# Two attention layers and two mixture-of-experts layers: shared expert's last 512 tokens behind the experts, tiles ordered by four levels, plain result rows

## What is computed

```python
scores = softmax(xt @ Wg.T)                      # 16 experts
# the 2 best of 4 groups, in them the 4 best experts of each token
h = silu(einsum('td,eid->eti', xt, W1)) * einsum('td,eid->eti', xt, W3)   # 176 inner values
y = einsum('etd,te->td', einsum('eti,edi->etd', h, W2), combine)
z = silu(xt @ Ws1.T) * (xt @ Ws3.T) @ Ws2.T      # shared expert, 352 inner values
x = x + y + z
```

## Time and profile before

| | us |
|---|---|
| median of 3 runs | 1341.67 |
| lowest, highest | 1340.03, 1342.01 |
| the profiled execution | 1353.53 |
| its span, first to last instruction | 1351.8 |
| TensorE busy | 1150.4 (85%) |
| VectorE busy | 876.2 (65%) |
| POOL busy | 688.8 (51%) |
| ScalarE busy | 541.6 (40%) |
| mean granted TensorE clock | 0.936 of full |

### The profile page before, as it was taken

The page is one execution under the profiler, slowest core; times in us unless marked ns, Lnnn a source line. Parts: engine busy times, 40 slices in busy tenths (PEclk is TensorE's granted clock), DMA queues, the critical chain, the costliest instruction groups (busy, mean ns, idle before and its releaser), DMA issues.

```text
span 1351.8 us, 26055 instructions
## 1 busy us (share of the span) xinstructions
PE 1150.4 (85%) x8706; PEld 615.6 (46%) x8706; DVE 876.2 (65%) x2067; ACT 541.6 (40%) x846; POOL 688.8 (51%) x841
## 2 busy tenths in 40 slices
PE   6888999998898899999287899999879878899990
PEld 2343444442654556566144344444247445565650
DVE  5578898991674345555389799999667524354543
ACT  2124777779520122222032477777844011222210
POOL 4352344444036577767453355454520656667671
PEclk9887999999988999999689899999998988899995
DMA  4424333320824679887745322121053347788868
GB/s 140 147 86 126 111 116 120 109 65 3 287 83 131 183 164 161 151 159 108 191 138 169 117 57 58 55 60 52 3 211 87 108 149 180 133 148 157 156 87 262
DMA packets 145875, 169.84 MB, mean 126 GB/s; under 512 B 20240, under 2 KB 130768, under 8 KB 145232
## 3 DMA queue, kind: packets, MB, share of 16 engines
q1 hardware_dynamic: 115856, 128.79, 32.8%
q0 software_dynamic: 29184, 38.36, 16.8%
q10 hardware_dynamic: 704, 1.02, 0.2%
HBM read 93.29 MB, written 76.18 MB: 125 GB/s over the span
## 4 chain that ended last, share of the span: by engine, by line
PE 57%; DVE 18%; DMA 7%; issue 6%; ACT 6%; SPq 2%; another core or an unknown queue 2%; POOL 2%; POOLq 0%; ACTq 0%; DVEq 0%
PE pair_ps L1992 10%; PE o_ps L1757 9%; ACT arena L845 4%; DVE nm L1119 4%; PE pair_ps L2025 4%; DMA x_slots<-y_sb,slot_i 4%; DVE bm L1119 3%; PE pair_ps L2028 2%; PE t_ps L1783 2%; PE pair_ps L1707 2%; PE pair_ps L1588 2%; PE pair_ps L1687 2%; PE pair_ps L1999 2%; PE pair_ps L1712 2%
## 5 line engine op out<-in xcount | busy, mean ns | idle before, releaser
L845 ACT ACTIVATE arena<-pair_ps 128x1024 f32<-128x1024 f32 x320 | 322.8, 1024 | 131.0 <-PE pair_ps L1682 76.1
L625 POOL TENSOR_SCALAR_AFFINE_SELECT arena<-arena 128x512 f32<-128x512 f32 (+1 forms) x320 | 174.9, 547 | 240.9 <-ACT arena L845 240.4
L1119 DVE TENSOR_REDUCE nm<-pair_ps 128x2 f32<-128x1024 f32 (+1 forms) x192 | 232.6, 1222 | 33.4 <-PE pair_ps L1731 29.6
L685 POOL DMA_INDIRECT x_slots<-y_sb,slot_i x128 | 123.9, 968 | 168.4 <-DVE slot_i L1317 89.9
L1757 PE MATMUL o_ps<-arena 128*9 128x512 f32 (+7 forms) x2048 | 177.0, 441 | 4.1 <-POOL arena L625 3.9
L1992 PE MATMUL pair_ps<-arena 128*128 x512 | 167.7, 469 | 2.4 <-ACT arena L896 2.4
L1119 DVE TENSOR_REDUCE bm<-pair_ps 128x8 f32<-128x1024 f32 x128 | 155.4, 1218 | 4.2 <-PE pair_ps L1731 1.0
L701 POOL DMA_INDIRECT y_h<-xnT,dest x80 | 125.3, 1566 | 53.5 <-DVE xnT L1476 25.2
L701 POOL DMA_INDIRECT y_f<-xnT,dest x80 | 124.6, 1558 | 44.6 <-issue 20.5
L1459 DVE TENSOR_TENSOR arena<-arena,pair_ps 128x128 f32<-128x128 f32 x144 | 41.4, 288 | 124.7 <-ACT arena L901 70.0
L1992 PEld LDWEIGHTS pair_ps<-arena 128*128 128x128 f32 x512 | 93.7, 194 | 43.6 <-issue 6.0
(11 more groups left out here) (275 smaller groups left out, 1999.7 us busy)
## 6 DMA issues: line engine op xcount, KB each, us to landing
arena<-x_slots SPq DMA_DIRECT2D x128, 132.5 KB
arena<-in_w SPq DMA_DIRECT2D x4, 2816.0 KB, 18.6
arena<-q_a SPq DMA_DIRECT2D x64, 96.0 KB
arena<-q_b SPq DMA_DIRECT2D x64, 96.0 KB
y_f<-hw SPq DMA_DIRECT2D x11, 512.0 KB, 2.9
y_h<-hw SPq DMA_DIRECT2D x11, 512.0 KB, 2.9
arena<-in_w SPq DMA_DIRECT2D x2, 2048.0 KB, 17.2
arena<-y_f SPq DMA_DIRECT2D x8, 512.0 KB
```

What stands on the lines that cost most here:

```text
L625: pool.affine_select(p, p, pattern, ALU.is_ge, 0.0, base=0, channel_multiplier=-1)\
L685: pool.indirect_dma_start(x_slots, bass.IndirectOffsetOnAxis(ap=slot_i[:, t, k:k + 1], axis=0), y_sb[:, t, :], None).then_inc(sm(f"scat{n ...
L845: act.activation(p_ring[:, U % RING, :], pair_ps[:, pair_at("T", n, u)].rearrange("p a c -> p (a c)"), ACT.Exp, scale=SCALE).then_inc(sm(" ...
L1119: dve.tensor_reduce(dst, src, X, ALU.max, negate=not 2 <= u < 4).then_inc(sm("t_max_done"), 1)
```

## The change

Three edits. **First**, the shared expert's chunks 9, 10 and 11 (the last batch of 512 tokens) run behind the last expert tile, on TensorE, ScalarE and VectorE; their sums go to the PSUM bank s_ps. In f, VectorE's part of them lies between the additions of the reload, and attention b's second batch waits on TensorE until they are added. **Second**, tiles are ordered by four levels: tile 0 waits for 24 scatters, tile 8 for 32, tile 16 for 40, tile 24 for 48 and tile 32 for 64; POOL keeps 24 scatters instead of 12 for the time of the experts, two behind each of the first 12 results; mixed tiles are 35, 39, ... 63. **Third**, each token has four rows of its own in one result tensor, so results are plain scatters of 72 tiles, without accumulation, without zero fills and without the store of x_sb. The reload is 8 DMAs of 1 MB into places that are free by then, the last two behind the last shared chunk; VectorE adds four rows per token (`dve_sum`), for two token tiles at a time, and POOL adds none. POOL's memset for the keys follows directly behind the last result. The output is stored in eight pieces. The diff, cut to its core:

```diff
-MIX = tuple(range(29, NJ, 6))
+MIX = tuple(range(35, 64, 4))
...
-ACCS = 3
 
 XR = 8
+Y_ROWS = ROWS * TOPK + P * XR
 WR = 6
-EARLY_T = 10
-EARLY = 24
-LATE_FIRST = 12
+LEVELS = (6, 8, 10, 12)
+NL = len(LEVELS)
+FIRST_X = 40
...
-        back = arena[:, o_p:o_p + NT * E].rearrange("p (t e) -> p t e", t=NT)
-        back2 = arena[:, o_p + NT * E:o_p + 2 * NT * E].rearrange("p (t e) -> p t e", t=NT)
+        back = [part.rearrange("p (u k e) -> p u k e", u=TB, k=TOPK) for part in
+                (arena[:, 0:T * 8], y_flat[:, 0:T * 8], arena[:, o_g:o_g + T * 8], arena[:, o_p:o_p + T * 8])]
...
-                if s == "a" and n < 22:
-                    f, a = "fh"[n % 2], 0 if n < 2 else 1 if n < 12 else 2
-                    first = ROWS if n < 2 else (n // 2 - 1) % 5 * 4 * P
-                    sp.dma_start(y_acc[f][a][first:first + 4 * P, :].rearrange("(a p) e -> p a e", p=P),
-                                 zero[:, 0:E].unsqueeze(1).to_broadcast([P, 4, E])).then_inc(sm("cleared"), 16)
...
-            for b in range(B - 1):
-                store_x(b)
             sp.wait_ge(sm("padded"), 16 * NE * (1 + past(f, 1)))
-            for parity in range(2):
-                sp.wait_ge(sm(f"scat{parity}"), 16 * (EARLY_T * TOPK // 2 + past(f, NT * TOPK // 2)))
...
-                if j == EARLY:
-                    for parity in range(2):
-                        sp.wait_ge(sm(f"scat{parity}"), 16 * (NT * TOPK // 2) * (1 + past(f, 1)))
+                for t, first in zip(LEVELS + (NT,), (0,) + tuple(TOPK * t - NE for t in LEVELS)):
+                    if j == first:
+                        for parity in range(2):
+                            sp.wait_ge(sm(f"scat{parity}"), 16 * (t * TOPK // 2 + past(f, NT * TOPK // 2)))
                 load(j)
...
-            sp.wait_ge(sm("store_second"), 16 * MIXED * (1 + past(f, 1)))
+            rows = y_rows[f][0:ROWS * TOPK, :].rearrange("(t p k) e -> p t k e", p=P, k=TOPK)
             for b in range(B):
-                for a, to in ((0, x_sb), (1, back), (2, back2)):
-                    rows = y_acc[f][a][b * T:(b + 1) * T, :].rearrange("(t p) e -> p t e", p=P)
-                    sp.dma_start(to[:, b * TB:(b + 1) * TB, :], rows).then_inc(sm(f"load{2 * b + a % 2}"), 16)
+                if b == B - 1:
+                    sp.wait_ge(sm(f + "_hw_used"), 3 * B + 2)
+                for u in (0, 2):
+                    sp.dma_start(back[b][:, u:u + 2], rows[:, b * TB + u:b * TB + u + 2])\
+                        .then_inc(sm(f"load{2 * b + u // 2}"), 16)
...
-            for b in range(B):
-                sp.wait_ge(sm("h_x"), (b + 1) * TB)
-                sp.dma_start(out_d[:, b * TB:(b + 1) * TB, :], x_sb[:, b * TB:(b + 1) * TB, :]).then_inc(sm("stored"), 16)
-            sp.wait_ge(sm("stored"), 16 * B)
+            for t in range(0, NT, 2):
+                sp.wait_ge(sm("h_x"), t + 2)
+                sp.dma_start(out_d[:, t:t + 2, :], x_sb[:, t:t + 2, :]).then_inc(sm("stored"), 16)
+            sp.wait_ge(sm("stored"), 16 * NT // 2)
...
-            outs = [(j, h) for j in range(NJ) for h in range(1 + (j in MIX))]
...
             def result_out(j):
                 pool.wait_ge(sm("e_dest"), j // 4 + 1 + past(f, NJ // 4))
                 pool.wait_ge(sm("e_y_ev"), j + 1 + past(f, NJ))
-                if j == 0:
-                    pool.wait_ge(sm("acc_x"), 16 * B * (1 + past(f, 1)))
-                scatter_out(outs.index((j, 0)))
-                if j in MIX:
-                    scatter_out(outs.index((j, 1)))
+                pool.indirect_dma_start(y_rows[f], bass.IndirectOffsetOnAxis(ap=dest[:, j:j + 1], axis=0),
+                                        yt[:, j % XR, :], None).then_inc(sm(f"store{j % XR}"), 16)
 
             pool.wait_ge(sm("e_slots"), 1 + past(f, 2))
-            pool.wait_ge(sm("cleared"), 16 * 23)
+            pool.wait_ge(sm("cleared"), 16)
             for n in range(TH * TOPK):
                 scatter(n)
             pool.wait_ge(sm("e_slots"), 2 + past(f, 2))
-            for n in range(TH * TOPK, EARLY_T * TOPK + LATE_FIRST):
+            for n in range(TH * TOPK, FIRST_X):
                 scatter(n)
-            late = range(EARLY_T * TOPK + LATE_FIRST, NT * TOPK)
+            late = range(FIRST_X, NT * TOPK)
...
+            for k in range(3 * (B - 1), 3 * B):
+                shared_silu(k)
...
                 for u in range(TB):
-                    dve_back(dve, "f", u)
+                    if u % 2 == 0:
+                        dve_weigh(dve, "f", 3 * (B - 1) + u // 2)
+                    dve_back(dve, u)
+                dve_weigh(dve, "f", 3 * B - 1)
                 dve_rstd(dve, 5, 2, 0, TB)
                 for u in range(TB):
                     dve_ln(dve, s, u)
+                dve_add_shared(dve, "f", B - 1)
                 dve.wait_ge(sm("b_w"), 112)
...
+        def dve_sum(dve, f, q):
+
+
+            b, u, t = q // 2, q % 2 * 2, 2 * q
+            done = q + 1 + past(f, 2 * B)
+            part = back[b][:, u:u + 2]
+            dve.wait_ge(sm(f"load{q}"), 16 * (loads(q) + past(f, loads(q))))
+            dve.tensor_tensor(part[:, :, 0:2, :], part[:, :, 0:2, :], part[:, :, 2:4, :], ALU.add).then_inc(sm("back_half"), 1)
+            dve.wait_ge(sm("back_half"), done)
+            dve.tensor_tensor(part[:, :, 0, :], part[:, :, 0, :], part[:, :, 1, :], ALU.add).then_inc(sm("back_sum"), 1)
+            dve.wait_ge(sm("back_sum"), done)
+            dve.wait_ge(sm("e_z_free"), TB * (b + 1) + past(f, NT))
+            dve.tensor_tensor(x_sb[:, t:t + 2, :], x_sb[:, t:t + 2, :], part[:, :, 0, :], ALU.add).then_inc(sm(f + "_x"), 2)
+
+        def dve_back(dve, t):
+
+
+            if t % 2 == 0:
+                dve_sum(dve, "f", t // 2)
+                dve.wait_ge(sm("f_x"), t + 2)
+            dve_stats(dve, 2, t)
+
+        def z_ps(b, u):
+
+
+            return (s_ps[:, u // 2] if b == B - 1 else t_ps if u < 2 else o_ps)[:, (u % 2) * E:(u % 2) * E + E]
+
+        def dve_add_shared(dve, f, b):
+            dve.wait_ge(sm(f + "_hw_used"), 3 * b + 3 + 2)
+            for u in range(TB):
+                t = TB * b + u
+                dve.tensor_tensor(x_sb[:, t, :], x_sb[:, t, :], z_ps(b, u), ALU.add).then_inc(sm("e_z_free"), 1)
+
+        def dve_weigh(dve, f, k):
+            m = SCH[k % 3][1]
+            dve.wait_ge(sm("e_sil"), k + 1 + past(f, 3 * B))
+            dve.wait_ge(sm(f + "_hw_used"), k + 1)
+            dve.tensor_tensor(hw[0:m, k % 2, :], sil[0:m, k % 2, :], st_ps[0:m, k % 2, 512:1024], ALU.mult)\
+                .then_inc(sm(f + "_sil_free"), 1)
...
-                ch(dve.tensor_copy(r[:, 4:5], s_ps[:, 1, 0:1]))
-                ch(dve.tensor_scalar(r[:, 5:6], r[:, 4:5], float(EARLY), lane_late, ALU.min, ALU.subtract))
-                ch(dve.tensor_scalar(r[:, 6:7], r[:, 4:5], float(EARLY), r[:, 3:4], ALU.is_lt, ALU.mult))
-                ch(dve.tensor_tensor(r[:, 7:8], r[:, 4:5], r[:, 5:6], ALU.add))
-                ch(dve.tensor_scalar(r[:, 7:8], r[:, 7:8], r[:, 6:7], r[:, 5:6], ALU.mult, ALU.subtract))
+                ch(dve.tensor_copy(lev_v[:, 0:1], lane))
+                ch(dve.tensor_copy(lev_v[:, 1:NL + 1], s_ps[:, 1, 0:NL]))
+                ch(dve.tensor_tensor(lev_d[:], s_ps[:, 1, NL:2 * NL], lev_v[:, 1:NL + 1], ALU.subtract))
+                ch(dve.tensor_tensor(lev_v[:, 0:NL], lev_v[:, 0:NL], lev_d[:], ALU.add))
+                ch(dve.tensor_tensor(lev_h[:], lev_f[:, 0:NL + 1], lev_f[:, 1:NL + 2], ALU.subtract))
+                ch(dve.tensor_tensor(lev_v[:], lev_v[:], lev_h[:], ALU.mult))
+                ch(dve.tensor_reduce(r[:, 7:8], lev_v[:], X, ALU.add))
...
-            for k in range(2, 3 * B):
-                weigh(k)
+            for k in range(2, 3 * (B - 1)):
+                dve_weigh(dve, f, k)
                 if k % 3 == 0:
-                    add_shared(k // 3 - 1)
...
+                    dve.scalar_tensor_tensor(dest[:, four], slot_w[:, four, 1], float(Y_ROWS), nowhere[:, q:q + 4], ALU.add, ALU.min)\
+                        .then_inc(sm("e_dest"), 1)
...
-            for t in range(NT):
-                dve_back(dve, "h", t)
+            for q in range(2 * B):
+                if q < 3:
+                    dve_weigh(dve, "h", 3 * (B - 1) + q)
+                dve_sum(dve, "h", q)
+                if q == 2:
+                    dve_add_shared(dve, "h", B - 1)
...
+                if s == "b" and b == 1:
+                    pe.wait_ge(sm("e_z_free"), NT)
...
+            pe.wait_ge(sm("e_y_ev"), NJ + past(f, NJ))
+            shared_in(3 * B - 3)
+            shared_in(3 * B - 2)
+            shared_out(3 * B - 3)
+            shared_in(3 * B - 1)
+            shared_out(3 * B - 2)
+            shared_out(3 * B - 1)
```

187 lines of the change are left out of this document (65 added, 122 removed).

## The result

The changed kernel took 1380.58 us (median of four, 1375.3 to 1387.99) beside 1340.85 us for the kernel before (1337.96 to 1342.01): ratio 1.029, interval 1.0235 to 1.0343. It is slower by 2.9%; 2% faster was forecast, and the time lies far outside the range of 1300 to 1328. Where some executions of a kernel were over 1.5% above its fastest, comparisons use the others alone.

What follows compares the result with a forecast made beforehand. TensorE, 85% busy, was taken to bound the later experts, with losses while POOL scatters and in the seams. Terms -14.5 - 15.0 + 2 + 0 + 0 + 0.3 = -27.2, off the median 1341.67, gave 1314 us; range 1300 to 1328.

Steps and rivals of the forecast that it cites:

- Part 1: Join of shared expert and experts: three shared chunks moved behind the experts start them earlier, -14.5 us in f, -15.0 in h.
- part 7: Cheap ones: zero fills 0 to -1 us, level arithmetic 0 to +1, TensorE's 5.5 us wait before the join -5 to +5.
- Part 3: Early experts beside POOL's scatters: TensorE's losses grow with the longer overlap, less traffic offsets; +2 us, bounds -6 and +8.
- Part 2: Results as plain rows: 0.98 plus 0.3 us each on POOL, last result lands 4.4 us earlier, 4.0 in f.
- No stall of the ring: Experts with late scatters: results lag by 17 us, which the ring of 8 result buffers covers with 19.
- Part 4: SP beside the mixed tiles, now 4 apart: 4 us of lag barely covered; 0, up to +3 us for both FFNs.
- Part 5: Seam into attention b: VectorE's extra additions less savings give +3.2 us, absorbed by its 3.44 us wait; 0, bounds -5 and +6.
- the 4 to 8 us that the prediction feared: Seam into attention b: up to eight VectorE additions slowed by POOL's splitting of the projections, 4 to 8 us worse.
- Part 6: The end: larger reload +6.0 us, earlier start -4.4, shorter tail -1.3; sum +0.3, bounds -3 and +3.
- (e): Rival: first part of the experts starves, slower once over 26 us an FFN is lost; 1358 us at 34 each; chance 0.03.
- (c): Rival: padding and order table come 5 us later than read and hold the join in both FFNs; 1324 us; chance 0.06.

Runs made afterwards that it cites:

- after_again: The changed kernel, unaltered, measured again on a quick chip: 1304.22 us, ratio 0.976 to the kernel before.
- before_again: The kernel before, unaltered, measured again on a quick chip: 1332.55 us, ratio 0.999 to the kernel before timed beside it.
- before_late24: Kernel before with 24 late scatters instead of 12, two behind each of the first 12 results, results still accumulating; slow chip: 1398.68 us, ratio 1.031.
- three_two: Changed kernel with three late scatters for every two of the first 16 results, instead of two for each of 12: 1296.07 us, ratio 0.971 to the kernel before.
- the later pair: Profiles of the kernel before and the changed kernel, both unaltered, taken later on chip 1: spans 1333.1 and 1303.0 us.

## Why the prediction was wrong, point by point

**Part 1, the join.** This is the first step that failed: -14.5 and -15.0 came out as -3.2 and -9.0. It took 15.5 us less work for TensorE as an earlier join, with nothing set aside for late hand-overs on the way. The reading of what TensorE has to do was right. In after_again the three chunks are gone from the stage without a loss; from POOL's first scatter to the last shared output it takes 45.8 us in both f and h, against 62.2 and 60.7 in before_again, 16.4 and 14.9 less. TensorE's timeline there, after_again and then before_again:

```profile
429.63 1.03 PE L1923 MATMUL o_ps<-arena,hw 96*128 96x256 f32 x4
432.35 0.63 PE L1945 MATMUL t_ps<-c_f,arena 128*128 128x128 f32 x4 [1.69 <-DVE arena L1439]
```

```profile
449.52 1.03 PE L1944 MATMUL o_ps<-arena,hw 96*128 96x256 f32 x4
456.50 0.66 PE L1967 MATMUL t_ps<-c_f,arena 128*128 128x128 f32 x2 [5.95 <-DMA arena<-x_slots]
```

On that quick chip the gain is even larger, since the old kernel's wait for loads behind the 40th scatter (5.95 us in f, 7.15 in h) goes too, which in the profile of the prediction was hidden behind a slow shared stage. On the slow chip the same stage took 68.6 and 64.1 us in the changed kernel, 23 and 18 more than on a quick chip, where the old kernel lost 8 and 12. The late hand-overs show there as well, to ACT and to VectorE; in the changed kernel, what the first three of these rows wait for had ended on TensorE at 423.3, 419.9 and 423.4 (ACT's SiLU, VectorE's addition of a batch, its order table, and the end of that table):

```profile
428.22 0.60 ACT L857 ACTIVATE sil<-pair_ps 128x512 f32<-128x512 f32 x1 [16.50 <-remote]
434.20 0.75 DVE L1235 TENSOR_TENSOR x_sb<-x_sb,t_ps 128x256 f32<-128x256 f32 x2 [4.66 <-remote]
444.66 0.24 DVE L1406 TENSOR_SCALAR tile_e<-pair_ps 128x80 int32<-128x80 f32 x1 [9.05 <-remote]
446.28 0.17 DVE L1412 TENSOR_SCALAR first_row<-arena 128x8 int32<-128x8 f32 x1
```

The prediction had seen one such pause, 5.5 us in the earlier trace rows, put it under part 7 as something that "can change", and gave it 5 us. It should have asked what the pause was: with less work between the scatters' start and the join, any pause in between stands on the path. The loads were late too. The table of tiles was ready at 446.5 instead of 436.9, the padding at 445.3 instead of 436.2, and the first load came at 447.8 instead of the forecast 439.5:

```profile
447.78 1.49 SPq L467 DMA_DIRECT2D arena<-x_slots  x2
```

With the prediction's 5.7 us from load to transpose, the join of f could not have come before 453.5, whatever TensorE did. In h the loads allowed it from 1126.1, 62.3 us behind POOL's first scatter, where the forecast has the join itself at 59.8. So both ends of the join were late, TensorE's and SP's. Why TensorE's loss grew from 8 and 12 to 23 and 18 is open.

**Part 3, the early experts.** The second failed step, and the larger: +2 for both FFNs, bounds -6 and +8, measured +19.1 and +17.0. The sign and the place were right. The step took the loss as a share of the time beside the scatters, and then took away for smaller traffic. More traffic was not the cause: the DMA share fell from 0.73 to 0.40 in h while the loss rose. What rose with it is the number of scatters beside the experts, 12 to 24; before_late24, the old kernel with that edit alone, is 3.1% slower on such a chip, in part beside the experts. By the number the loss would have been forecast as 8.5 and 14.5 doubled, +23 in all; measured is +36. So neither the share of time nor the number of scatters gives its size.

**Part 2, the results.** Right in size (0.96 + 0.30 = 1.26 us each). The last result lands 4.9 us after the last expert matmul in h (1350.26 - 1345.3) against 8.5 before: 3.6 earlier for 4.4. "No stall of the ring", 17 us of lag for 19 of cover, was wrong by a little: on quick chips TensorE waits 3.6 us in f and 3.2 in h for VectorE behind a full ring, and three_two, which spreads the scatters over 16 tiles, ends that and is 8 us faster.

**Part 4, SP beside the mixed tiles.** Right at 0: from 530 on TensorE was busy 130.00 of 130 us.

**Part 5, the seam into attention b.** Forecast 0 (-5 to +6), measured +5.3 and +4.5. The size of the additions was right:

```profile
676.63 1.22 DVE L1211 TENSOR_TENSOR arena<-arena 128x1024 f32<-128x1024 f32 x1 [3.92 <-DMA arena<-y_f]
...
705.77 0.69 DVE L969 TENSOR_TENSOR arena<-pair_ps,arena 128x512 f32<-128x512 f32 x1 [3.90 <-ACT arena L745]
```

(the changed kernel, VectorE). 1.22 for 1024 elements was forecast as 1.2, and in the later pair the first addition comes 10.0 us behind the last matmul instead of 15.5, for the 5.4 of the sum. But VectorE's wait for ACT ahead of the 512 column addition, which was to take up 3.4 us, is still there with 3.90. It belongs to the order of work and is not slack; without that credit the sum is +3.2. Another 2.0 are what the prediction had only named as a danger, without a term: additions beside POOL's splits of the projections. Four are stretched, from 0.69 to 0.98, 1.47 and 1.52 and from 1.22 to 1.29, and POOL's with them, in the quick trace as in the slow:

```profile
708.70 1.47 DVE L1216 TENSOR_TENSOR x_sb<-x_sb,arena 128x512 f32<-128x512 f32 x1
713.21 1.52 DVE L1213 TENSOR_TENSOR arena<-arena 128x512 f32<-128x512 f32 x1
712.17 2.01 POOL L590 TENSOR_TENSOR arena<-arena 128x512 bf16<-128x512 f32 x1
```

Together that is +5.2. (The 4 to 8 us that the prediction feared could not all have been "inside the bounds", which ended at +6.)

**Part 6, the end.** +0.9 for +0.3, though not as described. The chain of waits of the changed kernel at the end:

```profile
1347.85 2.41 DMA y_h<-xnT,dest
1350.36 5.16 DMA arena<-y_h
1355.54 1.24 DVE arena L1211
...
1377.83 0.70 DVE arena L1213
```

VectorE adds without a break from 1355.5; the reload is early enough, and 8.4 MB at 350 GB/s don't set the end. The number was right by luck: terms that cancelled hid this.

**Part 7.** Zero fills: start to the first scatter of f is 385.1 against 386.4 us, and 384.8 against 388.4 in the later pair; over all traces it lies between 384.8 and 390.1, so no gain can be read from it. Level arithmetic cost nothing: on the quick chip the table of tiles is ready 39.0 us behind the first scatter, 39.9 before.

**The sum.** Forecast -27.2, measured +30.1: 57.3 apart, of which 17.3 are the joins, 34.1 the experts, 5.3 the seam, 0.6 the end. On a quick chip the same sum gives -30.1 (profiled spans 1303.0 and 1333.1), 2.9 from the forecast, though with the joins 15 us better and the rest worse, so that closeness is in part luck.

**The rivals.** What came was (e), given 0.03: TensorE's loss passed its point of 26 us an FFN with 28 and 35. It was priced at 1358 for 34 us each, with the join's gain kept; the join failed as well, by the same kind of pause, and (e) had not put the two together. Rival (c), padding and order table late, came too, in f: 9 us, not 5. All three go with late hand-overs and a slow SP while POOL scatters; they should have been one rival. The argument against (e), "the worst stretch shows 27%", was drawn from one execution on one chip.
